# A gated cross-attention block: values kept on chip, keys made four steps ahead, keys and queries stacked by SBUF-to-SBUF copies

## The reference

```
q = (layernorm(x) @ Wq.T) * 32**-0.5        x: 16 x 224 x 512, 16 heads of 32
k = ctx @ Wk.T ; v = ctx @ Wv.T             ctx: 16 x 750 x 512
x = x + tanh(g0) * (sigmoid(q k^T) v) @ Wo.T
tokens = layernorm(x), 8 experts of 448 tokens (2 batches each)
x = x + tanh(g1) * (gelu(tokens @ w1[e] + b1[e]) @ w2[e] + b2[e])     w1: 512 x 2048, w2: 2048 x 512
```

## Time and profile before

| | |
|---|---|
| time, median of three runs | 1877.3 us (1871.76 to 1879.54) |
| span of the profiled execution, first to last instruction | 1868.1 us (its own device time is not listed apart from the three) |
| TensorE matmul busy | 1786.9 us, 96% |
| ScalarE, VectorE, GpSimd busy | 774.4, 692.1, 268.9 us |
| mean granted clock of TensorE | 0.98 |
| mean of one: ScalarE's sigmoid (L689), its copy of a V block (L719), its split of a context chunk (L675) | 1.67, 0.59, 1.03 us |
| mean of one: VectorE's split of a context chunk (L812), a small layernorm step (L29 to L31), a large one (L836) | 1.20, 0.16, 0.54 us |
| moved by DMA | 356.8 MB, 191 GB/s over the span |

### The profile page before, as it was taken

One profiled execution on the slowest core, in us unless ns is written; L12 is line 12 of the kernel. 1 busy time (PEld: TensorE's weight loads), 2 busy tenths in 40 slices (PEclk: granted clock), 3 DMA queues, 4 the chain that ended last, 5 costly groups with the idle time before them and its releaser, 6 DMA issues.

```text
span 1868.1 us, 35544 instructions
## 1 busy us (share of the span) xinstructions
PE 1786.9 (96%) x12672; PEld 1527.1 (82%) x12672; DVE 692.1 (37%) x1320; ACT 774.4 (41%) x1004; POOL 268.9 (14%) x397
## 2 busy tenths in 40 slices
PE   7899999999999999999999998799999999999998
PEld 7678787887887787877877876589999999999997
DVE  5223323233232232233232331255453544545453
ACT  4444454444444443544444443533333333333331
POOL 2222122222221221222222221000000000000000
PEclk9899999999999999999999998899999999999999
DMA  7988879798898888898898988743543535343451
GB/s 243 220 219 234 218 225 231 205 252 210 222 247 205 229 230 210 223 247 198 243 243 196 246 216 199 181 142 114 169 133 108 174 111 158 125 149 132 124 169 41
DMA packets 239490, 356.82 MB, mean 191 GB/s; under 512 B 19536, under 2 KB 162000, under 8 KB 239440
## 3 DMA queue, kind: packets, MB, share of 16 engines
q1 hardware_dynamic: 205504, 246.61, 53.1%
q0 software_dynamic: 33936, 109.54, 18.0%
HBM read 245.65 MB, written 110.43 MB: 191 GB/s over the span
## 4 chain that ended last, share of the span: by engine, by line
PE 83%; DMA 12%; SPq 2%; ACT 1%; DVE 1%; issue 1%; POOLq 0%; DVEq 0%; ACTq 0%
PE fill_ps L468 34%; PE scores_ps L625 17%; PE fill_ps L607 17%; PE heads_ps L517 7%; DMA v_sb<-v_scr 7%; PE scores_ps L501 7%; DMA v_scr<-v_stage 2%; DMA q_st<-q_scr 2%; SPq L269 1%; PE fill_ps L567 1%; ACT v_stage L719 0%; SPq L339 0%; ACT probs L689 0%; DMA k_scr<-k_stage 0%; PE fill_ps L641 0%
## 5 line engine op out<-in xcount | busy, mean ns | idle before, releaser
L689 ACT ACTIVATE probs<-scores_ps 125x1792 f32<-125x1792 f32 x192 | 319.9, 1666 | 219.2 <-PE scores_ps L501 219.2
L607 PE MATMUL fill_ps<-wQ,wK 128*128 128x448 f32 x1536 | 331.2, 369 | 0.0
L625 PE MATMUL scores_ps<-ctx_hl,wV 128*128 128x448 f32 x1536 | 324.5, 367 | 0.8 <-ACT x1nT L723 0.8
L468 PE MATMUL fill_ps<-ctx_hl,wK 128*128 128x250 f32 x2304 | 306.0, 283 | 9.1 <-DVE wK L818 8.7
L607 PEld LDWEIGHTS fill_ps<-wQ,wK 128*128 128x128 f32 x1536 | 287.9, 189 | 27.1 <-issue 1.1
L625 PEld LDWEIGHTS scores_ps<-ctx_hl,wV 128*128 128x128 f32 x1536 | 287.0, 187 | 28.0 <-issue 0.9
L468 PEld LDWEIGHTS fill_ps<-ctx_hl,wK 128*128 128x128 f32 x2304 | 286.2, 192 | 14.9 <-issue 13.7
L468 PE MATMUL fill_ps<-wV,ctx_hl 128*125 128x512 f32 x1152 | 292.1, 402 | 0.0
L468 PEld LDWEIGHTS fill_ps<-wV,ctx_hl 128*125 128x125 f32 x1152 | 206.1, 185 | 77.2 <-issue 31.5
L517 PE MATMUL heads_ps<-probs,v_sb 125*32 125x224 f32 x3072 | 191.1, 368 | 46.9 <-DMA v_sb<-v_scr 46.0
L868 DVE TENSOR_TENSOR k_stage<-fill_ps,k_stage 128x250 fp32r<-128x250 f32 x192 | 79.9, 417 | 406.1 <-ACT k_stage L713 404.6
(11 more groups left out here) (78 smaller groups left out, 1201.8 us busy)
## 6 DMA issues: line engine op xcount, KB each, us to landing
k_st<-k_scr SPq DMA_DIRECT2D x192, 375.0 KB, 7.7
w_raw<-w_in SPq DMA_DIRECT2D x128, 512.0 KB, 4.4
k_scr<-k_stage POOLq DMA_DIRECT2D x192, 250.0 KB, 7.2
ctx_raw<-ctxT_in SPq DMA_DIRECT2D x48, 500.0 KB, 9.0
v_scr<-v_stage POOLq DMA_DIRECT2D x96, 250.0 KB, 6.2
v_sb<-v_scr SPq DMA_DIRECT2D x64, 375.0 KB
q_st<-q_scr SPq DMA_DIRECT2D x192, 112.0 KB, 8.5
q_scr<-q_stage POOLq DMA_DIRECT2D x64, 224.0 KB, 6.4
```

Source lines behind the costliest of these rows:

```text
L468: last = pe.matmul(out_, lhsT(kt, a), rhs(kt, c), start=(kt == 0 and t == 0), stop=(kt == KT - 1 and t == 2))
L607: last = pe.matmul(hid_ps[k][:, 0:T], w1[:, slot, a, kt, k * P:(k + 1) * P], xt[:, d, kt, :], start=(kt == 0 and t == 0), stop=(kt == KT - ...
L625: last = pe.matmul(y_ps[:, dt, 0:T], w2[:, slot, a, k, dt * P:(dt + 1) * P], hid_hl[:, slot, d, k, :], start=(c == 0 and k == 0 and t == 0 ...
L689: nc.scalar.activation(probs[0:ST, s % 2], scores_ps[0:ST, :, 0:2 * L], ACT.Sigmoid, scale=SCALE).then_inc(s_probs, 1)
```

## The change

Five things are done at once.

1. **Values** stay on chip. `v_sb` now holds all values of two batches (the one in use and the next); ScalarE writes them there out of PSUM (`leave_v`). The six stores and four loads a batch are gone.
2. **Keys** are made four steps ahead and are laid out by step, not by chunk: the K block of step s makes what `scores` needs at step s+4. `k_st3` has four slots of 250 columns, and the three stacked copies for four heads are 12 transfers of 32 partitions by 1000 B from `k_stage`, on SyncE's queue (`spread_k`), behind two waits.
3. **Queries** are stacked in the same way by 12 transfers of 32 partitions by 896 B, on GpSimd's queue (`spread_q`). Q 1, 2 and 3 are now made within their own batch, at steps 1, 4 and 7, and needed at steps 3, 6 and 9; Q 0 is made at step 10 for step 0 of the next batch.
4. **Heads** are visited four times a batch, at steps 3, 6, 9 and step 0 of the next, with 24 matmuls (48 instructions) each; `probs` has three buffers.
5. **Rows of 4 KB**: context, projection weights and expert weights are laid out by the host so that a partition's part of a transfer is one contiguous row. Context has two raw buffers.

The second layernorm is cut in two over steps 3 and 4, `x1n` takes the place of `x_res`, the start prepares less (four K, five V, one Q) and the last batch more.

```diff
+    FILL = [(0, "K", 0), (0, "V", 5), (1, "Q", 1), (1, "K", 1), (1, "O", 0), (2, "K", 2), (2, "O", 1), (3, "K", 3),
+            (4, "Q", 2), (4, "K", 4), (5, "K", 5), (5, "U", 0), (5, "U", 1), (6, "K", 6), (7, "Q", 3), (7, "K", 7),
+            (7, "V", 0), (8, "T", 0), (8, "T", 1), (8, "K", 8), (8, "V", 1), (9, "K", 9), (9, "V", 2),
+            (10, "Q", 0), (10, "K", 10), (10, "V", 3), (11, "K", 11), (11, "V", 4)]
+    FILL_FIRST = [(0, "K", 8), (1, "K", 11), (2, "V", 0), (3, "V", 1), (4, "K", 9), (5, "V", 2), (6, "T", 0), (6, "T", 1),
+                  (7, "K", 10), (8, "Q", 0), (9, "V", 3), (10, "V", 4)]
+    CTX_SPLITS = {6: 0, 7: 1, 9: 2}
...
+            def spread_k(b, i):
+                r = i % 4
+                alone(sp, done["K"], nth("K", b, i))
+                alone(sp, s_scores, STEPS * b + i + 1)
+                for j in range(HEADS):
+                    for t, half in enumerate((HI, LO, HI)):
+                        sp.dma_start(k_st3[t * HD:(t + 1) * HD, r, j, :].bitcast(F32),
+                                     k_stage[j * HD:(j + 1) * HD, r, half, :].bitcast(F32)).then_inc(s_k_in[r], 16)
...
-                        pool.dma_start(scr["v"][bass.ds(n, 1), i * ST:(i + 1) * ST, :]
-                                       .rearrange("a p d -> p (a d)"), v_stage[0:ST, i % 2]).then_inc(s_v_st[i % 2], 16)
...
+            def spread_q(b, i):
+                n, r = target(b, "Q", i), i % 2
+                alone(pool, done["Q"], nth("Q", b, i))
+
+                alone(pool, s_scores, STEPS * n + 3 * (i - 2) + 3)
+                for j in range(HEADS):
+                    for t, half in enumerate((HI, HI, LO)):
+                        pool.dma_start(q_st3[t * HD:(t + 1) * HD, r, j, :].bitcast(F32),
+                                       q_stage[j * HD:(j + 1) * HD, r, half, :].bitcast(F32)).then_inc(s_q_in[r], 16)
...
+            def heads(b, par, mt):
+
+                if mt == 0:
+                    pe.wait_ge(done["V"], 6 * (b + 1))
+
+                at(pe, s_o_lo, KT * b + mt)
+                pe.wait_ge(s_probs, STEPS * b + 3 * mt + 3)
+                for pair in range(3):
+                    for t in range(2):
+                        for j in range(HEADS):
+                            last = pe.matmul(heads_ps[j * HD:(j + 1) * HD, 0:L],
+                                             v_sb[0:ST, par, 2 * pair + t, mt * P + j * HD:mt * P + (j + 1) * HD],
+                                             probs[0:ST, pair, j, t * L:(t + 1) * L],
+                                             start=(pair == 0 and t == 0), stop=(pair == 2 and t == 1))
+                    last.then_inc(s_av, 1)
...
+                    if follows(b) and s in (3, 4):
+                        ln_x1(b, *((0,) if s == 3 else (1, 2)))
...
+        "ctxT": np.asarray(ctx_1024).reshape(B, 3, S // 3, 4, 128).transpose(0, 1, 4, 3, 2).reshape(B, 3, 128, 4 * S // 3),
```

More of the change, by code:

```diff
@@ L70, in flamingo_block @@
[L70 to L74, removed]
+    assert T == NB * L and TT == LT and NB == 2 and KT == 4 and T <= 512 and C % 2 == 0 and C >= 4 and E >= 3
@@ L86, in known, with fills @@
     def known(b, value):
         return isinstance(b, int) and b == value
[L89 to L95, removed]
+    def fills(b):
+        if known(b, -1):
+            return FILL_FIRST
+        if known(b, 0):
+            return [f for f in FILL if f[1] not in "OU"]
+        if known(b, B - 1):
+            return [f for f in FILL if f[1] in "OU" or (f[1] in "KQ" and 0 < f[2] < 8) or f[1:] in (("K", 0), ("V", 5))]
+        if known(b, B):
+            return [f for f in FILL if f[1] in "OU"]
+        return FILL
@@ L105, in follows, with prepares @@
         return not isinstance(b, int) or b > 0
[L107 to L114, removed]
+    def prepares(b, ahead=1):
+        return not isinstance(b, int) or b + ahead < B
     def own(eng):
@@ L273, in load_v @@
[L273 to L280, removed]
-            def load_w(n):
[L283 to L289, removed]
@@ L504, in scores @@
                 last.then_inc(s_scores, 1)
-            def heads(b, s):
-                mt, pair = s // 3, s % 3
-                slot = mt % 2
-                if pair == 0:
-                    pe.wait_ge(s_v_in[slot], 16 * (2 * b + mt // 2 + 1))
-                    at(pe, s_o_lo, KT * b + mt)
-                pe.wait_ge(s_probs, STEPS * b + s + 1)
-                for t in range(2):
-                    for j in range(HEADS):
-                        last = pe.matmul(heads_ps[j * HD:(j + 1) * HD, 0:L],
-                                         v_sb[:, slot, 2 * pair + t, j * HD:(j + 1) * HD],
-                                         probs[0:ST, s % 2, j, t * L:(t + 1) * L],
-                                         start=(pair == 0 and t == 0), stop=(pair == 2 and t == 1))
-                last.then_inc(s_av, 1)
@@ L724, in leave, with leave_v, body @@
                                    ps[:, 0:KT * LT].rearrange("p (t l) -> p t l", l=LT)).then_inc(done["U"], 1)
-            def body(b, prep, out_, ahead):
+            def leave_v(b, par, i):
+                n, place = target(b, "V", i), par if i == 5 else 1 - par
+                act.wait_ge(full["V"], nth("V", b, i))
+                at(act, s_av, STEPS * (n - 1))
+                if known(n, 1) and i == 0:
+                    act.wait_ge(s_w_lo, 2 * len(w))
+                nc.scalar.copy(v_sb[0:ST, place, i, :], fill_bank(b, "V", i)[0:ST, :]).then_inc(done["V"], 1)
+            def body(b, h, par):
+                nh, npar = (h, 1) if par == 0 else (h + 1, 0)
                 for s in range(STEPS):
@@ L729, in body @@
                         sigmoid(b, s)
-                    for kind, i in fill_at(b, prep, out_, s, "A"):
-                        leave(b, kind, i)
                     if s == 0 and follows(b):
```

427 lines of the change are left out of this document (210 added, 217 removed), and 7 rows, old and new, of the table FILL.

## The result

The changed kernel takes 2298.8 us (median of four runs, 2295.2 to 2299.9) against 1876.1 us before in the same series: ratio 1.225, 95% interval 1.219 to 1.230. The forecast had the sign, and the size was wrong: the time lies 309 us above the end of the range.

What follows compares the result with a forecast made beforehand. TensorE was taken to bound the kernel: 67.2 us of work plus query lateness, split and clock gave 75.6 a batch against 73.0. Span 1868.1 - 15 + 4 + 37 + 4 = 1898, plus 9.2 is 1907 us; range 1840 to 1990.

Steps and rivals of the forecast that it cites:

- Keys and SyncE's queue: Key copies on SyncE's queue: 144 x 0.48 = 69.1 plus 3.7, 72.8 us a batch, busy nearly throughout but not the bound.
- rival 4: SyncE's queue becomes the bound: at 0.55 an issue 83 us a batch, time 2010; decides from 0.50; chance 0.07.
- The prediction's own sign of being wrong: Issues over 0.5 from start to start on SyncE's queue with the wait at k_st, or under 0.4 on GpSimd.
- The queries' way: Query block to scores by twelve GpSimd issues of 0.50 and landing 2.2: needs 9.6, cover 4.4, Q 2 5.2 us late.
- The wait for U: At step 5 TensorE reaches U 1.9 us before the second layernorm's VectorE work ends; passes inside the 5.2 of Q 2.
- TensorE's work: TensorE's blocks in a batch of the new kernel sum to 67.2 us, against 68.4 for the old without wait and clock.
- Visits: Eight fewer heads visits a batch are worth 1.2 us of TensorE's work, bounds 0 and 2.5.
- Split of chunk 2: At step 9 the split stands behind V 2's copy on ScalarE and K 10 needs it: 0.75 us lost.
- Ends: Before batch 0 15 us saved (bounds 8 and 18), batch 0 at 77 and batch 15 each +4, experts 0.
- The 9.2 us between span and median: Median of the runs taken as 9.2 us above the profiled span, added to the span 1898 for 1907.
- Rows of 4 KB: 4 KB rows for weights give nothing in the experts, since nothing waits for them; at most 6 us.
- Values on chip: Heads' wait for values from DRAM, 46.0 us in all or 3.1 a batch, goes, with 1.5 a batch of half clock.

Runs made afterwards that it cites:

- e1: Kernel without the computation, twelve transfers of each kind back to back on an idle core: within SBUF 0.62 to 0.63 us each, load or store 0.45 with 32 rows.
- e9: e6 with each key's stack loaded from DRAM in twelve loads, one per head and term, and not three: 2009.4 us, ratio 1.066.
- e2: Changed kernel without two of the three stacked copies of each key, so scores hold one term of three: 1969.7 us, ratio 1.045.
- e4: Changed kernel with keys by DRAM again, one store a step and three loads, in the new order of work: 1950.6 us, ratio 1.035.
- e6: Changed kernel with both e4's keys by DRAM and e5's order of blocks: 1810.2 us, ratio 0.964.
- e10: e6 with T at the end of step 8, behind K 8 and V 1: 1793.4 us, ratio 0.952.
- e7: e6 with twelve visits of heads a batch and not four: 1810.9 us, ratio 0.964.
- e5: Changed kernel with Q 1, 2, 3, 0 at steps 0, 2, 5, 9 and the split of context chunk 2 at step 8: 2307.0 us, ratio 1.228.
- e8: e6 with the layouts of before for context and expert weights, projection weights keeping the new one: 1813.5 us, ratio 0.966.
- e11: Kernel before with V 4 and V 5 at step 8 and Q 1 and Q 2 at steps 9 and 10: 1852.6 us, ratio 0.984.

## Why the prediction was right in sign and wrong in size

**The step that failed** is "Keys and SyncE's queue": the term 144 x 0.48 = 69.1 for the queue. The mechanism stood there, with rival 4, and only its price was off. 0.48 came from the earlier trace rows, loads from DRAM, and I took it for the copies without a bound above, though the trace before has no copy within SBUF. e1 has 0.63 for them on an idle core. The sum that gave 72.8 comes out at 102.0 over batches 1 to 13 of the changed kernel, 29 more: 144 issues at 0.627 are 90.3 and not 69.1; the long ones, which nothing had foreseen and whose cause is open, add 4.2; the five loads and 24 waits with the gaps around them are 7.5 and not 3.7, 1.1 of it the gap at every second batch. So the price by itself, 0.63 for 0.48, is 21 of the 29, and enough to make the queue the bound. From 75.6 forecast to 100.5 measured, 15 batches carry 374 of the 392 us by which the forecast was off. The prediction's own sign of being wrong, over 0.5 on SyncE's queue with the wait at k_st, is what came.

Rival 4 was priced at 0.55 a piece, 83 us a batch and 2010 us. e9 took 83.0 and 2009, but that it fits so well is luck: 0.52 a piece and 9 us of the rest, where rival 4 has 3.7. Its chance of 0.07 was the second error: it said itself that it decides from 0.50, with the term at 0.48 and no row of the kind. I was careful about the queue whose price I knew to be unknown, GpSimd's, and not about the one whose price I thought I had read.

**The queries' way** was right in its mechanism and in most of its terms, hidden in the changed kernel and laid bare by e2 and e4. GpSimd's issue: 0.50 taken, between a slope and the nearest row, 0.498 measured. Landing: 2.2 taken, 2.07 by the prediction's other estimate, 1.8 in the median. The wait for U 1.9 and 1.9. Q 2 then late by another 3.3 forecast; 2.4 in the mean of e2 (2.33 above), 3.3 in that of e4, where GpSimd's queue also stores the keys (4.21 in the batch looked at). Its sum was too small all the same: 79.9 in e2 and not 75.6. In the mean of e2's batches 1 to 14 the bank that T holds costs 1.2, which the sum had not; Q 1 is 1.2 late and Q 0 0.9, where 0.2 and nothing had been forecast; Q 2 gives 0.9 back; the clock and TensorE's work are the other 2. With the queue out of the way e2 took 1970 and e4 1951, inside the range and 63 and 44 above the 1907. So the sign was not luck: queries late at step 6 make the kernel slower than before by themselves. But in the changed kernel it is another mechanism that made it slower.

**TensorE's work**, 67.2 forecast: without its idle time a batch is 68.1 in e6 and 67.9 in e10. Visits: 1.2 forecast; by e6 and e7 1.7, and 0 in time. **Split of chunk 2**: 0.75 forecast, 0.63 in e2; the 36.8 us in the changed kernel are its chunk's load standing behind key copies in the full queue, and in e5 this lateness moves to the sigmoid. **Ends**: first scores near 40 forecast, 42.8; batch 0 77 forecast, 80.3 in e2; the experts 652 forecast, 653. The 9.2 us between span and median were no fixed cost: in every later run the time lies 1.7 above the profiled span, so the profiled execution of before was some 7 us faster than the median. **Rows of 4 KB**: nothing forecast; e8 shows nothing that can be told. **Values on chip**: the wait is gone in all versions; e11 shows that a part of it was order.

**Where the expected gain went.** It was there. The change gives 3.6% once the keys don't go through 144 issues and the queries and the split come early enough (e6), 4.8% with T moved (e10). Of its parts, the four visits and the 4 KB rows of context and expert weights give nothing that can be told (e7, e8); values on chip and the lead of four steps were not taken apart from each other. The change lost it with the choice to stack keys within SBUF, and a smaller part with queries made late: with the keys by DRAM and the old order it is still 3.5% slower than before (e4).

## What to carry to other kernels

Count the issues on each queue and price each kind by its own two ends before anything else; a queue in order is an engine, and its sum belongs beside TensorE's. Where no row shows a kind of transfer, the sum needs a bound above as well as a value. Replacing a store and a load by DRAM by twelve copies within SBUF shortens the way and lengthens the queue, and the queue was the bound. A repair that gives nothing may only be standing behind a fuller resource: e5's order was worth nothing before e4 and 7% after it. And a wait that has gone from the list may have moved to another line, so look at all of them.

## What the runs showed of the hardware that was not expected

A transfer with both ends in SBUF cost the issuing queue of SyncE 0.61 to 0.63 us, with 32 rows or 128 and with 1000 or 4000 B in a row, and that of ScalarE 0.63; a load or store on SyncE's queue cost 0.45 with 32 rows and 0.48 to 0.49 with 128 (e1). GpSimd's queue issued the copy of 32 rows in 0.50 (e1) and 0.498 in the full kernel, so for such copies it was the quicker. In the full kernels a few issues took 0.9 us and more: 90 of 2304 in the changed kernel, 1.32 in the mean, and 80 of 2304 in e9, whose transfers are loads; in e1 none did. Their cause is open.
